# Experts' results scattered to token rows by Pool while the slots run, read back by plain loads; two DRAM rows a channel for keys and queries

## What is computed

```python
x = x + tanh(g_xattn[0]) * L0_xattn(layernorm(x), ctx, ctx, mask)     # 16 heads of 16, masked
x = x + tanh(g_ffn[0])   * L0_ffn(layernorm(x))
x = x + tanh(g_xattn[1]) * L1_xattn(layernorm(x), ctx)                # 16 heads of 16, no mask
x = x + tanh(g_ffn[1])   * L1_ffn(layernorm(x))
...
# L0_ffn: one of 8 experts for each token, 256 -> 1024 -> 256
idx = argmax(xf @ Wg, axis=-1)
for e in range(8):
    final += where(idx == e, (gelu(xf @ W1[e]) * (xf @ W2[e])) @ W3[e], 0)
return shared + final
...
# L1_ffn: two of 8 experts for each token, 256 -> 192 -> 256, weighted
scores = sigmoid(x @ W_gate_router)
_, sel = top_k(scores + expert_bias, 2)
w = scores at sel, divided by their sum
return shared + sum over the two of w * (silu(x @ Wg[e]) * (x @ Wu[e])) @ Wd[e]
```

## Time and profile before

| | us |
|---|---|
| median of 3 runs (lowest, highest) | 1796.72 (1796.28, 1798.78) |
| the profiled execution, its time | 1804.55 |
| its span in the trace | 1802.8 |

### The profile page before, as it was taken

The page is one execution under the profiler, slowest core; times in us unless marked ns, Lnnn a source line. Parts: engine busy times, 40 slices in busy tenths (PEclk is TensorE's granted clock), DMA queues, the critical chain, the costliest instruction groups (busy, mean ns, idle before and its releaser), DMA issues. The chain is left out here.

```text
span 1802.8 us, 23804 instructions
## 1 busy us (share of the span) xinstructions
PE 1484.4 (82%) x7833; PEld 870.4 (48%) x7834; DVE 1172.1 (65%) x2309; ACT 853.5 (47%) x1537; POOL 139.7 (8%) x248
## 2 busy tenths in 40 slices
PE   4658999869896999992499999999999997848870
PEld 3323333458785888882153333433433434725540
DVE  5738999463112777766399999999999946502335
ACT  3214777521212565641217777777777783211110
POOL 2000000002000000003100000000000000161116
PEclk9787999969998999996659999999999998779995
DMA  8954222120004899961722221112111100533114
GB/s 299 401 190 115 49 55 55 50 71 33 15 1 180 297 344 335 340 241 50 222 70 70 44 38 33 24 24 43 28 23 24 24 1 1 133 111 108 44 47 137
DMA packets 108715, 196.88 MB, mean 109 GB/s; under 512 B 9006, under 2 KB 80419, under 8 KB 108615
## 3 DMA queue, kind: packets, MB, share of 16 engines
q1 hardware_dynamic: 99377, 167.59, 30.0%
q0 software_dynamic: 6912, 25.71, 4.1%
q10 hardware_dynamic: 2326, 2.31, 0.4%
HBM read 144.69 MB, written 50.36 MB: 108 GB/s over the span
## 5 line engine op out<-in xcount | busy, mean ns | idle before, releaser
L1096 DVE TENSOR_REDUCE attend_piece_max<-attend_p_bank 128x1 f32<-128x400 f32 (+3 forms) x1280 | 668.7, 588 | 68.5 <-PE attend_p_bank L979 56.2
L1076 ACT ACTIVATE attend_probs<-attend_s_bank 128x512 f32<-128x512 f32 (+1 forms) x1053 | 549.4, 605 | 232.6 <-PE attend_s_bank L993 232.3
L979 PE MATMUL attend_p_bank<-attend_k_st,attend_q_st 62*128 62x400 f32 (+2 forms) x1280 | 416.3, 435 | 54.5 <-DMA attend_k_st<-ones_rows 50.0
L993 PE MATMUL attend_s_bank<-attend_q_st,attend_k_st 64*128 64x512 f32 (+1 forms) x1053 | 390.4, 446 | 28.3 <-ACT attend_probs L1076 13.9
L993 PEld LDWEIGHTS attend_s_bank<-attend_q_st,attend_k_st 64*128 64x128 f32 (+1 forms) x1053 | 167.8, 183 | 335.0 <-ACT attend_probs L1076 327.3
L1010 PE MATMUL attend_o_bank<-attend_probs,attend_v_st 128*32 128x512 f32 (+1 forms) x2176 | 290.9, 607 | 2.2 <-ACT attend_probs L1076 2.1
L979 PEld LDWEIGHTS attend_p_bank<-attend_k_st,attend_q_st 62*128 62x128 f32 x1280 | 209.1, 194 | 103.6 <-issue 52.0
L1713 DVE TENSOR_TENSOR slots_w_low<-slots_w_up,slots_w_high 128x2048 fp32r<-128x2048 f32 x46 | 105.1, 2287 | 46.2 <-ACT slots_w_high L1709 46.2
L1523 DVE TENSOR_TENSOR share_hid<-share_b_bank,share_g_act 128x512 f32<-128x512 f32 (+1 forms) x40 | 27.6, 691 | 123.7 <-PE share_b_bank L1374 103.2
L1709 ACT ACTIVATE slots_w_high<-slots_w_up 128x2048 fp32r<-128x2048 f32 x46 | 87.7, 1909 | 6.2 <-DMA slots_w_up<-in_L_ffn_W_dram 6.1
L1669 PE MATMUL slots_y_bank<-slots_w_dn,slots_hid_t 128*128 128x256 f32 x368 | 83.2, 379 | 1.0 <-DVE slots_hid_t L1720 1.0
(11 more groups left out here) (250 smaller groups left out, 1786.5 us busy)
## 6 DMA issues: line engine op xcount, KB each, us to landing
slots_w_up<-in_L_ffn_W_dram SPq DMA_DIRECT2D x46, 1024.0 KB, 7.5
slots_w_dn<-in_L_ffn_W_dram SPq DMA_DIRECT2D x23, 1024.0 KB, 5.8
prep_raw<-in_mask_BxSxS_ik_dram POOLq DMA_DIRECT2D x16, 800.5 KB, 9.8
attend_q_st<-q_rows SPq DMA_DIRECT2D x64, 192.0 KB, 4.8
k_rows<-prep_k_part SPq DMA_DIRECT2D x12, 800.5 KB, 7.7
attend_k_st<-k_rows SPq DMA_DIRECT2D x32, 300.2 KB, 5.8
q_rows<-prep_q_part SPq DMA_DIRECT2D x12, 512.0 KB, 11.2
sorted<-keep_zeros SPq DMA_DIRECT2D x6, 1024.0 KB
```

What stands on the lines that cost most here:

```text
L979: last = pe.matmul(bank[:, 0:even(kn)], q_st[rows, slot, t * P:(t + 1) * P].bitcast(F32R), k_st[rows, slot, k0:k0 + even(kn)].bitcast(F32R ...
L993: last = pe.matmul(out, k_st[rows, hs, kt * P:kt * P + kn].bitcast(F32R), q_st[rows, hs, q0:q0 + CH].bitcast(F32R), start=True, stop=not m ...
L1076: act.activation(probs[0:kn, (kt + hs) % RING, q0:q0 + CH], score_bank(i, h, hs, kt, c)[0:kn, :], ACT.Exp).then_inc(exp_done, 1)
L1096: dve.tensor_reduce(dst, bank_of(i, n)[:, 0:kn], AX.X, ALU.max).then_inc(entry_done, 1)
```

## The change

It has three parts.

1. **Two DRAM rows a channel.** `k_rows` and `q_rows` hold high and low once. The stores of prepare fall from 12 to 8 of 800.5 KB and from 12 to 8 of 512 KB, those of project_queries from 12 to 8. `load` in attend issues eight DMAs a head for the same SBUF bytes: for each half of the tokens, 32 partitions of k (high, low), 16 more of k (high again), 32 of q where both come from one DRAM row, 16 of q (low).
2. **A row carries its destination.** Sorted rows are 272 floats (`ROW`) in place of 256; float 256 holds the number of the row in `back` that the result goes to: 1 + token for the first choice, 1 + 2048 + token for the second, and 0 (the zero fill) where the slot's row is empty. In route_and_share Pool writes these numbers into `x_n`; in layer 1 it rewrites them four tiles at a time for the second choice, each time behind a wait for the first choice's scatters of these tiles.
3. **Results go to token rows at once.** In both slot stages Pool works out the target (an empty row gets a spare row of its own behind the real ones) and scatters each slot's result with one indirect DMA (23 and 39); SP's stores are gone. In layer 1 the order on Pool is `send(s - 5)`, which waits for that slot's copied result, and then the stage copy of slot s. Pool also adds `acc` to `x_now` in four operations of 128x1024 (layer 0 behind the first two `aim`, layer 1 at the last four slots). `acc` is now scaled with the gate by ACT where it leaves PSUM, and the weights of layer 1 by DVE. collect has SP's plain loads of 512 KB, 4 in layer 0 and 8 in layer 1, and DVE does one operation for each tile and choice (and the statistics in layer 0).

The diff, cut to its core; `const["index"]` is a constant made by Pool at the start (128 by 71: token rows, then spare rows):

```diff
-                for row, part in ((0, 0), (2, 0), (1, 1)):
-                    if part == 0:
-                        sp.wait_ge(k_high, NP * (u + 1))
-                    else:
-                        sp.wait_ge(k_low, NP * (u + 1))
-                    sp.dma_start(scratch["k"][l, b * P:(b + 1) * P, row], k_part[:, u % KR, part])\
-                        .then_inc(k_stored[u], 16)
+                sp.wait_ge(k_high, NP * (u + 1))
+                sp.dma_start(scratch["k"][l, b * P:(b + 1) * P, 0], k_part[:, u % KR, 0]).then_inc(k_stored[u], 16)
+                sp.wait_ge(k_low, NP * (u + 1))
+                sp.dma_start(scratch["k"][l, b * P:(b + 1) * P, 1], k_part[:, u % KR, 1]).then_inc(k_stored[u], 16)
             def store_queries(n):
...
-                    at = slice(a * SIDE, a * SIDE + DATA)
-                    sp.dma_start(k_st[at, slot, 0:S],
+                    both, rest = (slice(a * SIDE + m, a * SIDE + n) for m, n in ((0, PART * DK), (PART * DK, DATA)))
+                    own = slice(a * HALF, (a + 1) * HALF)
+                    sp.dma_start(k_st[both, slot, 0:S],
                                  scratch["k"][l, channels, :, keys.slice(0, S)].rearrange("d r s -> (d r) s"))\
                         .then_inc(landed, 16)
-                    sp.dma_start(q_st[at, slot],
-                                 scratch["q"][channels, :, a * HALF:(a + 1) * HALF].rearrange("d r q -> (d r) q"))\
+                    sp.dma_start(k_st[rest, slot, 0:S], scratch["k"][l, channels, 0, keys.slice(0, S)])\
                         .then_inc(landed, 16)
+                    sp.dma_start(q_st[both, slot],
+                                 scratch["q"][channels, 0, own].unsqueeze(1).to_broadcast([DK, PART, HALF]))\
+                        .then_inc(landed, 16)
+                    sp.dma_start(q_st[rest, slot], scratch["q"][channels, 1, own]).then_inc(landed, 16)
...
+            pool.memset(x_n[:, :, D:ROW], 0.0).then_inc(numbered, 1)
+            pool.wait_ge(numbered, 1)
             for k in range(K):
+                if k == 0:
+                    pool.tensor_copy(x_n[:, :, D], const["index"][:, 0:QT]).then_inc(numbered, 1)
                 pool.wait_ge(placed, k + 1)
                 for t in range(QT):
+                    g = t // 4
+                    if k and t % 4 == 0:
+                        pool.wait_ge(scattered[g], 64 * k)
+                        pool.tensor_copy(x_n[:, t:t + 4, D], const["index"][:, k * QT + t:k * QT + t + 4])\
+                            .then_inc(numbered, 1)
+                    if t % 4 == 0:
+                        pool.wait_ge(numbered, 2 if k == 0 else 2 + 4 * (k - 1) + g + 1)
                     pool.indirect_dma_start(scratch["sorted"][l][:, :],
                                             bass.IndirectOffsetOnAxis(ap=place[:, k, t:t + 1], axis=0),
-                                            x_n[:, t], None).then_inc(scattered, 16)
-            pool.wait_ge(scattered, 16 * K * QT)
+                                            x_n[:, t], None).then_inc(scattered[g], 16)
+            for g in range(4):
+                pool.wait_ge(scattered[g], 64 * K)
...
+                    act.activation(acc[:, n], y_bank[n % 2][:, :], ACT.Copy, scale=const["gates"][:, 2 + l:3 + l])\
+                            .then_inc(y_copied, 1)
...
-            def store(s, slot):
-                sp.dma_start(scratch["back"][l][bass.ds(s * P, P), :], y_sb[:, slot]).then_inc(y_stored[slot], 16)
-
...
-                wait(sp, y_copied, s + 1)
-                store(s, s % 2)
-                if s == NS - 3:
-                    load_down(NS - 1, (NS - 1) % 2)
+            sp.wait_ge(y_copied, NS - 2)
+            load_down(NS - 1, (NS - 1) % 2)
+
+        @block.gpsimd
+        def _(pool):
+            def aim(s):
+
+                slot, spare = s % 2, const["index"][:, m.K * QT + s:m.K * QT + s + 1]
+                pool.wait_ge(rows_in[slot], (s - slot) * 8 + 16)
+                pool.tensor_scalar(index[:, s:s + 1], rows[:, slot, D:D + 1], 0.0, spare, ALU.is_equal, ALU.mult)\
+                    .then_inc(indexed, 1)
+                pool.wait_ge(indexed, 2 * s + 1)
+                pool.tensor_tensor(index[:, s:s + 1], index[:, s:s + 1], rows[:, slot, D:D + 1], ALU.add)\
+                    .then_inc(indexed, 1)
+                pool.wait_ge(indexed, 2 * s + 2)
+                pool.tensor_copy(target[:, s:s + 1], index[:, s:s + 1]).then_inc(aimed, 1)
+
+            aim(0)
+            aim(1)
+            for t in range(0, QT, 4):
+                pool.tensor_tensor(x_now[:, t:t + 4], x_now[:, t:t + 4], acc[:, t:t + 4], ALU.add).then_inc(summed, 1)
+            for s in range(NS):
+                if s + 2 < NS:
+                    aim(s + 2)
+                pool.wait_ge(y_copied, s + 1)
+                pool.wait_ge(aimed, s + 1)
+                pool.indirect_dma_start(scratch["back"][l][:, :],
+                                        bass.IndirectOffsetOnAxis(ap=target[:, s:s + 1], axis=0), y_sb[:, s % 2], None)\
+                    .then_inc(y_stored[s % 2], 16)
             for n in range(2):
-                sp.wait_ge(y_stored[n], 16 * ((NS + 1 - n) // 2))
+                pool.wait_ge(y_stored[n], 16 * ((NS + 1 - n) // 2))
         @block.tensor
         def _(pe):
...
-            def body(s, k):
-                if again(s):
-                    wait(pool, x_turned, s - 1, apart=True)
-                pool.tensor_copy(stage[:, k], rows[:, bass.ds(s, 1)].rearrange("p a d -> p (a d)")).then_inc(staged, 1)
+            def stage_rows(s):
+                if s >= 2:
+                    pool.wait_ge(x_turned, s - 1)
+                pool.tensor_copy(stage[:, s % 2], rows[:, s, 0:D]).then_inc(staged, 1)
+
+            def aim(a, b, done):
+
+                pool.tensor_scalar(index[:, a:b], rows[:, a:b, D], 0.0, None, ALU.is_equal).then_inc(indexed, 1)
+                pool.wait_ge(indexed, done + 1)
+                pool.tensor_tensor(index[:, a:b], index[:, a:b], const["index"][:, m.K * QT + a:m.K * QT + b], ALU.mult)\
+                    .then_inc(indexed, 1)
+                pool.wait_ge(indexed, done + 2)
+                pool.tensor_tensor(index[:, a:b], index[:, a:b], rows[:, a:b, D], ALU.add).then_inc(indexed, 1)
+                pool.wait_ge(indexed, done + 3)
+                pool.tensor_copy(target[:, a:b], index[:, a:b]).then_inc(indexed, 1)
+
+            def send(s):
+                pool.wait_ge(y_copied, s + 1)
+                pool.indirect_dma_start(scratch["back"][l][:, :],
+                                        bass.IndirectOffsetOnAxis(ap=target[:, s:s + 1], axis=0), y[:, s], None)\
+                    .then_inc(y_stored, 16)
             pool.wait_ge(head_in, 16)
-            for s in range(HEAD):
-                body(s, s % 2)
+            for s in range(HEAD - 1):
+                stage_rows(s)
+            aim(0, HEAD, 0)
+            stage_rows(HEAD - 1)
+            pool.wait_ge(indexed, 4)
+            send(0)
             pool.wait_ge(rest_in, 16 * -(-(NS - HEAD) // 12))
-            with pool.Fori(HEAD, NS - 1, 2) as j:
-                for u in range(2):
-                    body(j + u, (HEAD + u) % 2)
+            stage_rows(HEAD)
+            aim(HEAD, NS, 4)
+            pool.wait_ge(indexed, 8)
+            for s in range(HEAD + 1, NS):
+                send(s - HEAD)
+                stage_rows(s)
+                if s >= NS - QT // 4:
+                    t = 4 * (s - NS + QT // 4)
+                    pool.tensor_tensor(x_now[:, t:t + 4], x_now[:, t:t + 4], acc[:, t:t + 4], ALU.add).then_inc(summed, 1)
+            for s in range(NS - HEAD, NS):
+                send(s)
+            pool.wait_ge(y_stored, 16 * NS)
...
         summed, final, stored, counted = sc.sem("summed"), sc.sem("final"), sc.sem("stored"), sc.sem("counted")
-        gathered = const["gathered"][l]
         block = ctx.enter_context(nc.Block())
-
-        @block.gpsimd
-        def _(pool):
-            for t in range(QT):
-                for k in range(K):
-                    pool.indirect_dma_start(back[:, k, t], None, scratch["back"][l][:, :],
-                                            bass.IndirectOffsetOnAxis(ap=place[:, k, t:t + 1], axis=0))\
-                        .then_inc(gathered[t], 16)
-            for t in range(QT):
-                pool.wait_ge(gathered[t], 16 * K)
         @block.sync
         def _(sp):
+            for n in range(4):
+                for k in range(K):
+                    a = 1 + k * T + 4 * n * P
+                    sp.dma_start(back[:, k, 4 * n:4 * n + 4],
...
+            if K == 1:
+                for t in range(QT + 1):
+                    if t < QT:
+                        dve.wait_ge(landed[t // 4], 16)
+                        add(t, 0, final)
+                    if t:
+                        dve.wait_ge(final, t)
+                        dve.bn_stats(stats[:, t - 1], x_now[:, t - 1]).then_inc(counted, 1)
```

(12 more changed lines are left out.)

117 lines of the change are left out of this document (55 added, 62 removed).

## The result

The changed kernel takes **1767.92 us** (median of 4 runs, 1766.11 to 1769.34) against 1796.78 for the one before (median of 4, 1796.28 to 1798.78): the ratio is 0.9837 [0.982, 0.9854], 28.9 us or 1.6% less. Predicted was 1765, between 1754 and 1778. The profiled execution took 1767.28 with a span of 1765.5. The total was met within 2.9 us, but partly by luck: two terms of the sum were far too small, and one that was put at nothing was large, with the other sign.

What follows compares the result with a forecast made beforehand. The prediction took the end as bound by Pool's 32 gathers in collect 1, with barrier-separated stages before; its terms summed to -31.5 us, giving 1773.0 from the profiled 1804.55 and 1765 from the median 1796.72, range 1754 to 1778.

Steps and rivals of the forecast that it cites:

- collect 1: Last stage: plain loads and independent additions replace 32 gathers on Pool, ending at 1776.5 in place of 1799.44: -23 us.
- collect 0: Layer 0's collect: DVE starts later but takes 0.77 us a tile, ending at 836.2 in place of 840.28: -4 us.
- prepare: First stage: fewer k and q stores shorten DVE's mask waits by 5 us and the last store's by 2: -7 us.
- attend loads: Attend 0: eight DMAs a head start the last load 1.6 us later; 0.15 us a head assumed: +2 us.
- attend starts: Start of each attend: 16 DMAs instead of 8 ahead of the values, against stores that end sooner: 0 (-4 to +4).
- slots 0: Layer 0's slot stage: Pool's four additions run where DVE makes the first slots_w_low: +1 us (0 to +6).
- slots 1: Layer 1's slot stage: send goes ahead of each stage copy, with 1.2 to 1.9 us margin left: 0 (0 to +2).
- The rival of loads at half rate: Collects: plain loads of just-written rows run at half the rate, collect 1 ends at 1784, +8: 1773 us; chance 0.06.
- the slower one: Slots 1: Pool's send becomes the bound and PE waits every slot; 1809 us at a 4.5 us send; chance 0.04.
- attend 0's load comes late: Attend 0: late loads cost some 0.8 us in 13 heads, 10 in place of 2: 1773 us; chance 0.17.
- the rival on the port: Slots 0: port contention puts DVE and PE behind Pool's additions, +6: 1770 us; chance 0.06.
- half way to the rival: Prepare: the rival has masks' waits partly DVE's own order, only the last store gone, -2 not -7: 1770 us; chance 0.14.

Runs made afterwards that it cites:

- The experiment with two queues: The changed kernel with attend 0's query loads issued on Pool's queue beside SP's key loads, four DMAs on each a head: 1775.41 us, ratio 0.9808.
- the last two experiments: The kernel before with one of two weighted additions a tile left out in collect 1: ratio 0.9989; and with 96 empty SP instructions after attend 0: 0.9994.

## Why the prediction was right or wrong

| term | predicted | measured | from |
|---|---|---|---|
| collect 1 | -23 | -22.2 | last result to last sum 48.3, 26.1 |
| collect 0 | -4 | -5.9 | 28.3, 22.4 |
| prepare | -7 | -4.1 | 128.7, 124.6 |
| project_queries | -2 | -2.3 | last q store to next load 7.2, 4.9 |
| attend loads | +2 | +7.4 | attend 0 207.1, 214.5 |
| attend starts | 0 | -7.7 | 11.2 to 8.1; 16.5 to 11.9 |
| route 1 | +1.5 | +1.2 | 83.95, 85.1 |
| slots 0 | +1 | +6.1 | 251.1, 257.2 |
| slots 1 | 0 | -1.2 | 129.7, 128.5: within what repeats vary |
| sum | -31.5 | -28.7 | -28.9 between the medians |

**The collects** were the case as written. In collect 1 the hand-over took 6.05 in place of 5.5 us, the first group 6.5 in place of 5.6, and the step 0.40 in place of 0.41. In collect 0 all three were somewhat better than forecast. That the gathers and not DVE's chain of dependent additions bounded the old collect 1 is borne out by the kernel with a third of the additions gone, worth 1.3 to 2.0 us of 49. The rival of loads at half rate did not come; nor did the slower one: a send in slots 1 takes 984 ns as the earlier trace rows suggested, and PE waits for no stage.

**Attend loads: the step that failed** is the choice of 0.15 a head in place of 0.8. The mistake stands ahead of it, in "the last starts 4 x 0.4 = 1.6 us later". In the kernel before a head's last load starts 1.30 us behind its first (213.28, 214.58), in the kernel after 3.74 (195.88, 199.62), so 2.44 later, since the new q loads cost SP 0.57 to 0.64 each. The landing was even shorter than assumed: from the start of the last load to the matmul it is 2.7 us. Before, there were 4.35 us for it (214.58 to 218.93), so 1.9 were left, and 2.7 - 1.9 = 0.8 is the wait of 0.73 that a head shows. The head grew by only 0.4, 16 of them are 6.2 of the 7.4 us, since another wait of PE shrank meanwhile, that for the maxima (in total, times, longest; first before, then after):

```profile
PE attend_p_bank L968 <- DVE keep_a_row_max L1130: 4.8, 15, 0.8
```

```profile
PE attend_p_bank L971 <- DVE keep_a_row_max L1133: 1.5, 2, 0.8
```

10.9 us of new waits less 3.3 are 7.6, about the 7.4 of the stage. It is the rival "attend 0's load comes late", at +7.4 where it had +10. By the Trainium skill (DMA: Bandwidth & Descriptors, section on rules for kernel authors), transfers under 64 KB mostly pay overhead; the prediction let the rule stand for +10 and took +2. The loads that PE waited for have 64 KB and landed in 2.6 us, the old ones of 192 KB in 3.5 (medians), so no slow landing shows. (The prediction also said that no run had a load that small; the kernel before has them, `attend_m_part` with 8 KB.) The experiment with two queues shows the overhead that counted here to be the issue: 10.9 us of waits went to none at equal sizes. The same section says that spreading DMAs over engines saves only sequencer issue time, and here the trace agrees: the head went from 12.14 to 11.74 us with the issue shared, although the landing went from 2.6 to 3.5.

**Slots 0: the step that failed** is the choice of +1 out of 0 to +6. The two first `slots_w_low` grew by 8.14 - 4.49 = 3.65 us, the third by 3.90 - 2.29 = 1.6. Leaving the additions out gave back 5.1 us of the stage, and moving them away gave back 4.0 with the sums kept. How the 5 us come about is seen between the kernel after and the one without the additions. PE's first product with a `slots_w_low` starts 1.6 us later behind the first load of the stage (14.9 and 13.3), and that of the next slot 2.5 us later (26.0 and 23.5), behind a wait of 3.5 us in place of 1.8. Behind this wait PE had a granted clock of 0.50, the level of 1.2 GHz, and the other kernel had 1.00, that of 2.4 (a stretch, its length, busy time of PE, PEld, DVE, ACT and Pool, clock, DMA share, GB/s; first after, then without the additions):

```profile
580.00:584.00 4.00, 4.00 (x11) 3.12 (x10) 2.21 (x1) 0.60 (x1) 0.07 (x1) 0.50 0.96 317
```

```profile
580.00:584.00 4.00, 4.00 (x25) 3.42 (x23) 2.14 (x4) 3.24 (x4) 0.00 (x0) 1.00 0.59 193
```

So about half of the 5 us are the later starts, and the other half is what the stage loses behind them, where the clock is low (by difference; no run separates the two). The kernel before has such a stretch too, at 0.73 from 584 to 588 us and 0.85 from there to 592. That is the rival on the port, in the size it was given (+6). The Trainium skill (SBUF — State Buffer, section on who interferes with whom) was right, by the 8.14 us in place of 4.49, and the prediction's discount of it had no row behind it: "nothing in the trace shows the two at once" was no evidence against.

**The attend starts** were left at 0 with 4 either way and brought -7.7. That is outside its own bounds, and the largest single miss. What moved is seen: with two rows, first load to first matmul went from 11.2 to 8.1 and from 16.5 to 11.9 us. With three rows in both layers both went back to the old size (11.3 and 17.7), with three rows in layer 0 only the first (11.3 and 10.6). Fewer stores alone do not do it: the kernel with two queues has as few of them, and its first start took 12.0. What that kernel changes is which queue issues the q loads. PE's first matmul of attend 1 with what it waited for, first before, then after:

```profile
894.07 1.04 PE L979 MATMUL attend_p_bank<-attend_k_st,attend_q_st 62*128 62x402 f32 x4 [26.59 <-DMA attend_k_st<-ones_rows]
```

```profile
878.89 1.03 PE L982 MATMUL attend_p_bank<-attend_k_st,attend_q_st 62*128 62x402 f32 x4 [19.38 <-DMA attend_q_st<-q_rows]
```

Before, the last to come was the load of `ones_rows` on another queue; after, it was q_rows. The small load was issued at 880.96 before and at 870.35 after. The DMA queues (packets, MB, share of the time) of the kernel before in 888 to 892, and of the kernel after in 870 to 874:

```profile
q1 hardware_dynamic: 462, 0.65, 95.1%
q10 hardware_dynamic: 14, 0.08, 10.0%
```

```profile
q1 hardware_dynamic: 188, 0.58, 96.4%
q10 hardware_dynamic: 5, 0.03, 6.4%
```

Before, the small queue (q10) moves its 16 packets from 888 to 894, 7 to 13 us behind the issue, 14 of them beside 462 of SP's in the stretch shown; after, it moves 16 from 872 to 878, 2 to 8 us behind the issue. That SP's queue, with four issues in place of two for the same bytes, left the small load an earlier place is read from this and was not tested by a run of its own.

**Prepare** gave -4.1 of -7 (the mean of six profiles of kernels with three rows in both layers is 129.4, of seven with two rows 124.9). The masks' waits fell by 3.5 where 5 were assumed: half way to the rival.

So the sum held because +5.4 and +5.1 too little were met by -7.7 and the smaller differences. That is luck: no step of the prediction ties them together. Choosing the median rather than the profiled 1804.55 as the base was right: by the traces, the 7.8 between them sat in route 0 (176.3 us, against 168.3 and 168.5 in the last two experiments). There, in the kernel before, ACT and DVE had these waits (in total, times, longest), and the kernel with three rows on one chip had such a one too:

```profile
ACT share_g_act L1411 <- remote: 12.0, 2, 6.4
...
DVE share_hid L1523 <- remote: 9.1, 1, 9.1
```

```profile
DVE share_hid L1560 <- remote: 8.3, 1, 8.3
```

The same program on another chip had none and took 168.7 in place of 176.0. Of the fourteen traces five have such waits and a route 0 of 175.7 to 176.3: the first of the kernel before and all four that were taken on one chip, whatever the kernel. The eight from two other chips and the first of the kernel after have none and 168.1 to 168.9. The stall thus goes with the chip, not with the change or the code. What makes it stays open.

## What to carry to other kernels

Replacing many indirect gathers at the end, where nothing covers them, by scatters under running matmuls and a few plain loads was worth 22.2 of 48.3 us here in one stage and 5.9 of 28.3 in the other. What stays can be priced beforehand: the hand-over (4.8 to 6.1 us from the last send to the first load), the first load (4.1 to 6.5) and the reader's own steps. Splitting a DMA inside a loop costs issue time on its queue, so put the measured issue of the new shape against the smallest margin of that loop, and give half of the DMAs to an idle engine's queue if it doesn't fit (but look at what stands ahead of them in the first rounds). Work handed to an idle Pool is not free when it meets two-input DVE operations; cut it into pieces that fit between them.

## What was not expected of the hardware

A scatter on Pool takes 2.68 us on the mean in slots 0 and 0.98 in slots 1, at equal bytes (groups of instructions of the kernel after):

```profile
L1662 POOL DMA_INDIRECT back<-slots_y_sb,slots_target x23 | 61.6, 2677 | 152.9 <-DVE slots_y_sb L1809 152.9
...
L1906 POOL DMA_INDIRECT back<-slots_y,slots_target x39 | 38.4, 984 | 59.4 <-DVE slots_y L2026 57.6 <-issue 1.3 <-POOL slots_target L1902 0.5
```

The timeline shows beside what: it starts 0.37 us into a `slots_w_low` and ends 0.92 behind it.

```profile
643.66 2.28 DVE L1753 TENSOR_TENSOR slots_w_low<-slots_w_up,slots_w_high 128x2048 fp32r<-128x2048 f32 x1
...
644.03 2.83 POOL L1662 DMA_INDIRECT back<-slots_y_sb,slots_target  x1 [6.31 <-DVE slots_y_sb L1809]
```

So do 21 of the 23, each 2.83 to 2.85 us long; the last two of the stage, with no `slots_w_low` beside them, take 0.98 and 0.97. The Trainium skill (SBUF — State Buffer, section on who interferes with whom) holds it for inferred that a two-input tensor operation does not stall the making of descriptors; these 21 scatters were held up by one. So the trace speaks against it, unless it was the reading of the 128 row numbers from `slots_target` that waited; no run separates the two. It cost little here: with the additions left out the sends stayed at 2.68 and the stage was at 252.2, against 251.1 before.

Pool's addition of 128x1024 takes 3.40 us in slots 0 and 2.36 in slots 1, of 128x256 0.76; a MEMSET of the large size took 0.95.
